# A graph network's gathers: one tile by single-row transfers before, two tiles and half of a third after, shared by two queues

## The reference

```python
h = relu(layernorm(x)); h = h @ enc_w + enc_b; h_list = [h]
for l in range(3):
    e = edge_attr @ edge_w[l] + edge_b[l]              # 16 -> 128
    msg = relu(h_list[l][src] + e)                     # a gather of 212,500 rows
    agg = segment_sum(msg, dst, num_segments=n_nodes)
    z = (1.0 + eps[l]) * h_list[l] + agg
    z = relu(z @ mlp_w1[l] + mlp_b1[l]) @ mlp_w2[l] + mlp_b2[l]
    h_list.append(relu(z))
out = x + (concatenate(h_list, axis=1) @ out_w + out_b)
```

## Time and profile before

| | us |
|---|---|
| median of 3 runs | 6243.44 |
| lowest, highest | 6243.08, 6244.88 |
| the profiled execution | 6233.49 |
| its span | 6231.7 |
| busy PE, PEld | 4832.8, 3004.4 |
| busy POOL | 4667.1 |
| busy DVE, ACT | 1645.1, 987.6 |

### The profile page before, as it was taken

The page is one execution under the profiler, slowest core; times in us unless marked ns, Lnnn a source line. Parts: engine busy times, 40 slices in busy tenths (PEclk is TensorE's granted clock), DMA queues, the critical chain, the costliest instruction groups (busy, mean ns, idle before and its releaser), DMA issues.

```text
span 6231.7 us, 86632 instructions
## 1 busy us (share of the span) xinstructions
PE 4832.8 (78%) x14396; PEld 3004.4 (48%) x14397; DVE 1645.1 (26%) x4181; ACT 987.6 (16%) x1583; POOL 4667.1 (75%) x4998
## 2 busy tenths in 40 slices
PE   7887777777777777777777777777777777777777
PEld 5554444444444444444444444444444444444444
DVE  6322222222222222222222222222222222222222
ACT  4111111111111111111111111111111111111111
POOL 6777777777777677777777777767777777777776
PEclk8555555555555555555555555555555555555555
DMA  4222222222222222222222222222222222222223
GB/s 140 66 64 64 62 64 64 64 64 62 64 64 64 63 63 64 63 63 64 64 64 64 62 64 64 64 62 61 60 61 61 61 61 60 61 61 60 59 60 96
DMA packets 209009, 408.00 MB, mean 65 GB/s; under 512 B 93779, under 2 KB 106684, under 8 KB 207948
## 3 DMA queue, kind: packets, MB, share of 16 engines
q0 software_dynamic: 156960, 321.77, 19.8%
q10 hardware_dynamic: 22096, 59.87, 3.3%
q1 hardware_dynamic: 29508, 22.58, 1.1%
HBM read 378.16 MB, written 25.69 MB: 65 GB/s over the span
## 4 chain that ended last, share of the span: by engine, by line
POOL 40%; PE 22%; issue 15%; DMA 14%; DVE 5%; ACT 4%; DVEq 0%; POOLq 0%; ACTq 0%
POOL rows L383 40%; DMA rows<-h_table,idx 14%; PE bank L634 14%; PE bank L630 6%; DVE rows L887 4%; ACT rows L551 4%; PE bank L653 0%; PE bank L655 0%; PE bank L608 0%; PE bank L600 0%; DVE onehot L751 0%; DMA out_acc<-x_t 0%; PE bank L593 0%; DVEq L957 0%; PE bank L661 0%
## 5 line engine op out<-in xcount | busy, mean ns | idle before, releaser
L383 POOL DMA_INDIRECT rows<-h_table,idx x4905 | 4630.1, 944 | 1525.8 <-issue 1266.7
L634 PEld LDWEIGHTS bank<-onehot,rows 128*128 128x128 f32 x9966 | 2087.3, 306 | 2784.9 <-ACT rows L551 2659.0
L634 PE MATMUL bank<-onehot,rows 128*128 128x64 f32 x9966 | 2235.3, 400 | 1347.8 <-ACT rows L551 1347.0
L630 PE MATMUL bank<-edgew,attr 65*128 65x512 f32 x2496 | 2235.2, 1008 | 9.3 <-DMA w2s<-w 9.3
L887 DVE TENSOR_TENSOR rows<-bank,rows 128x512 f32<-128x512 f32 x1248 | 861.0, 690 | 4037.0 <-DMA rows<-h_table,idx 3913.5
L551 ACT ACTIVATE rows<-rows 128x512 f32<-128x512 f32 x1248 | 784.3, 628 | 5156.6 <-DVE rows L887 5156.6
L630 PEld LDWEIGHTS bank<-edgew,attr 65*128 65x128 f32 x2496 | 665.0, 310 | 270.2 <-issue 270.2
L873 DVE TENSOR_TENSOR onehot<-bank,dst_rel 128x256 f32<-128x256 f32 x1248 | 518.1, 415 | 204.7 <-issue 204.7
L883 DVE TENSOR_TENSOR agg_t<-bank,agg_t 128x64 f32 x1248 | 269.6, 216 | 288.6 <-PE bank L634 288.4
L653 PE MATMUL bank<-agg_t,w1s 128*128 (+1 forms) x150 | 149.2, 1098 | 1.5 <-DVE agg_t L883 1.5
L674 PE MATMUL bank<-outw,h_t 128*128 128x128 f32 x588 | 148.8, 396 | 0.7 <-ACT h_t L514 0.7
(11 more groups left out here) (82 smaller groups left out, 459.6 us busy)
## 6 DMA issues: line engine op xcount, KB each, us to landing
rows<-h_table SPq DMA_DIRECT2D x9984, 0.5 KB
rows<-h_table,idx POOLq DMA_INDIRECT x4905, 2.5
attr<-ea_t ACTq DMA_DIRECT2D x155, 256.0 KB, 3.6
h_table<-h_n ACTq DMA_DIRECT2D x48, 256.0 KB, 2.1
h_table<-rows SPq DMA_DIRECT2D x24, 256.0 KB, 2.7
out<-out_acc SPq DMA_DIRECT2D x24, 256.0 KB, 3.1
out_acc<-x_t ACTq DMA_DIRECT2D x4, 1280.0 KB, 16.7
rows<-dst_g SPq DMA_DIRECT2D x1, 832.0 KB
```

The source lines that it names most:

```text
L383: return g.indirect_dma_start(dst, None, h_table[l % 2], bass.IndirectOffsetOnAxis(ap=index, axis=0))
L630: return nc.tensor.matmul(dst[0:EP, 0:tiles * D], cols, edgew[:, l, 0:tiles * D], start=True, stop=True)
L634: last = nc.tensor.matmul(dst[:, 0:WIN], rows[0:EP, slot, j, :], onehot[0:EP, hot_slot, j, :], start=(j == 0), stop=(j == tiles - 1))
```

## The change

- The row numbers come as `row_at`, three rows of them for three tiles of each round, and DVE multiplies them by 512 once, ahead of `s_ready`. The registers then hold byte addresses, and the table is seen as bytes (`h_bytes`), so that no address is computed for a row.
- SP now brings 176 rows of a round: rows 0 to 47 of the fourth tile of group 13, and all 128 of the fourth tile of group 14, in chunks of 16 with a load of 16 registers ahead of each.
- ACT brings 144 rows of a round, behind its relus, in chunks of at most 12: rows 48 to 127 of group 13's tile behind the relus of groups 0 to 6, and rows 64 to 127 of the fourth tile of group 15 behind those of groups 7 to 12. The last round has no such part of group 15.
- POOL gathers 62 tiles in a full round instead of 63, one of them with 64 rows.
- DVE waits for `shared_fetched`, `sync_fetched` and `half_fetched` at groups 13, 14 and 15.
- The 24 results of layer 2 are written to `out` by ACT, behind the relu of group 5 of each half (`store_out`), no longer by SP at the end. ACT waits for the end of the layer before (`stored`) ahead of each layer's first group.

```diff
-FK, FJ = 14, 3
-LOADS = 32
+SYNC_GROUP, SHARED_GROUP = 14, 13
+SHARED_BY_SYNC = 48
+CHUNK = 16
+ACT_ROWS = 12
+HALF_GROUP = 15
+BY_POOL = 64
...
+        def table_row(l, eng, at):
+            byte = eng.snap(at, donate=True, min_val=0, max_val=(NR * P - 1) * (D * 4))
+            return h_bytes[l % 2][bass.ds(byte, D * 4)].rearrange("(a d) -> a d", a=1)
...
-                def fetch_tile(b):
-                    for first in range(0, EP, LOADS):
-                        sp.load(row, row_idx[0:1, bass.ds(b * EP + first, LOADS)])
-                        for i in range(LOADS):
-                            at = sp.snap(row[i], min_val=0, max_val=NR * P - 1)
-                            sp.dma_start(rows[first + i:first + i + 1, FK, FJ, :], table[bass.ds(at, 1), :])\
-                              .then_inc(fetched, 16)
+                def fetch_rows(b, u, group, count, fetched):
+                    for first in range(0, count, CHUNK):
+                        with ExitStack() as held:
+                            at = [held.enter_context(sp.register(f"sync_at{next(named)}")) for _ in range(CHUNK)]
+                            sp.load(at, row_at[u:u + 1, bass.ds(b * EP + first, CHUNK)])
+                            for i in range(CHUNK):
+                                row = rows[first + i:first + i + 1, group, TG - 1, :]
+                                sp.dma_start(row.bitcast(u8), table_row(l, sp, at[i])).then_inc(fetched, 16)
+
+                def fetch_body(b):
...
+                    freed(SHARED_GROUP)
+                    fetch_rows(b, 1, SHARED_GROUP, SHARED_BY_SYNC, shared_fetched)
+                    freed(SYNC_GROUP)
+                    fetch_rows(b, 0, SYNC_GROUP, EP, sync_fetched)
...
-            with sp.Fori(0, ND) as i:
-                sp.wait_ge(o_added, i + ((L - 1) * NU + 1 + N0))
-                sp.dma_start(out[:, bass.ds(i * (UT * D), UT * D)].rearrange("p (t d) -> p t d", d=D),
-                             out_acc[:, bass.ds(i * UT, UT), :]).then_inc(s_out, 16)
...
-                    tiles = min(TG, NTR - group * TG) - (slot == FK)
-                    if slot != FK and tiles < TG:
+                    tiles = min(TG, NTR - group * TG)
+                    if slot in (SYNC_GROUP, SHARED_GROUP):
+                        tiles = TG - 1
+                    elif tiles < TG:
...
-                        gather(l, rows[0:EP, slot, t % TG, :], idx[0:EP, t:t + 1]).then_inc(gathered[slot], 16)
+                        here = BY_POOL if slot == HALF_GROUP and t % TG == TG - 1 else EP
+                        gather(l, rows[0:here, slot, t % TG, :], idx[0:here, t:t + 1]).then_inc(gathered[slot], 16)
...
+                def fetch_some(b, k):
+                    shared = -(-(EP - SHARED_BY_SYNC) // ACT_ROWS)
+                    if k < shared:
+                        first = SHARED_BY_SYNC + k * ACT_ROWS
+                        fetch_rows(b, 1, SHARED_GROUP, first, min(first + ACT_ROWS, EP), shared_fetched)
+                    elif not isinstance(b, int):
+                        first = BY_POOL + (k - shared) * ACT_ROWS
+                        if k == shared:
+                            wait_apart(act, agg_done, b * RING + (l * NG + HALF_GROUP + 1 + S0 - RING))
+                        if first < EP:
+                            fetch_rows(b, 2, HALF_GROUP, first, min(first + ACT_ROWS, EP), half_fetched)
...
+                        if k == 0 and not (isinstance(b, int) and b == 0 and l == 0):
+                            wait_apart(act, agg_done, b * RING + (l * NG + SHARED_GROUP + 1 + S0 - RING))
+                        fetch_some(b, k)
+
+                act.wait_ge(stored, l * NU * 16 + 16)
...
+                dve.wait_ge(row_at_in, 48)
+                own(v.tensor_scalar(row_at[:, :], row_at[:, :], float(D * 4), None, ALU.mult))
                 dve.sem_inc(s_ready, 1)
```

More of the change, by code:

```diff
@@ L3 @@
 from contextlib import ExitStack
+import itertools
 P = 128
@@ L54, in gnn_kernel @@
     assert ND * UT + LAST == -(-nodes // P) and NB == -(-NG // HB) and NGP <= P * GR and NI <= NBU
-    assert REST == RING and FK < RING - 1 and EP % LOADS == 0
+    assert REST == RING and EP % CHUNK == 0 and SHARED_BY_SYNC % CHUNK == 0
+    assert (EP - SHARED_BY_SYNC) // ACT_ROWS + 1 < SHARED_GROUP < SYNC_GROUP < HALF_GROUP == RING - 1 and GL < TG
     h_table = [nc.dram_tensor(f"h_table{u}", (NR * P, D), f32).ap() for u in range(2)]
@@ L59, in gnn_kernel @@
     h_last = [h[ND * UC:NR * P, :].rearrange("(p j) d -> p (j d)", j=LAST) for h in h_table]
+    h_bytes = [h.rearrange("n d -> (n d)").bitcast(u8) for h in h_table]
     spans_dram = nc.dram_tensor("spans", (2, NGP), i32).ap()
@@ L307, in _ @@
                     sp.dma_start(outb[:, :], out_b.partition_broadcast(P)).then_inc(s_par, 16)
-            row = [sp.alloc_register(f"row{i}") for i in range(LOADS)]
+            named = itertools.count()
             for l in range(L):
-                table = h_table[l % 2]
                 def far_pass():
@@ L317, in far_pass, with freed @@
                         sp.dma_start(far_attr[0:KA - 1, :], ea_t[:, bass.ds(g * EP, EP)]).then_inc(f_attr, 16)
-                def fetch_tile(b):
-                    for first in range(0, EP, LOADS):
-                        sp.load(row, row_idx[0:1, bass.ds(b * EP + first, LOADS)])
-                        for i in range(LOADS):
-                            at = sp.snap(row[i], min_val=0, max_val=NR * P - 1)
-                            sp.dma_start(rows[first + i:first + i + 1, FK, FJ, :], table[bass.ds(at, 1), :])\
-                              .then_inc(fetched, 16)
+                def fetch_rows(b, u, group, count, fetched):
[7 more added lines that the diff above has]
+                def fetch_body(b):
+                    def freed(group):
+                        before = l * NG + group + 1 + S0 - RING
+                        if not isinstance(b, int):
+                            wait_apart(sp, agg_done, b * RING + before)
+                        elif b or l:
+                            sp.wait_ge(agg_done, b * RING + before)
+                    freed(SHARED_GROUP)
+                    fetch_rows(b, 1, SHARED_GROUP, SHARED_BY_SYNC, shared_fetched)
+                    freed(SYNC_GROUP)
+                    fetch_rows(b, 0, SYNC_GROUP, EP, sync_fetched)
                 if l == 0:
@@ L491, in _ @@
             n_far = load_extra(act)
+            for u in range(4):
+                act.wait_ge(p_stored[u], (NI + 3 - u) // 4 * 16)
+            named = itertools.count()
             def load_weights(l):
@@ L515, in relu_h, with store_out @@
                       .then_inc(h_ready, 1)
+                def store_out(i):
+                    act.wait_ge(o_added, i + (l * NU + 1 + N0))
+                    act.dma_start(out[:, bass.ds(i * (UT * D), UT * D)].rearrange("p (t d) -> p t d", d=D),
+                                  out_acc[:, bass.ds(i * UT, UT), :]).then_inc(s_out, 16)
                 def store(i):
@@ L541, in load_next_attr, with fetch_rows @@
                            .then_inc(attr_in[1 - half], 16)
+                def fetch_rows(b, u, group, first, stop, fetched):
+                    with ExitStack() as held:
+                        at = [held.enter_context(act.register(f"act_at{next(named)}")) for _ in range(first, stop)]
+                        act.load(at, row_at[u:u + 1, bass.ds(b * EP + first, stop - first)])
+                        for i in range(first, stop):
+                            row = rows[i:i + 1, group, TG - 1, :]
+                            act.dma_start(row.bitcast(u8), table_row(l, act, at[i - first])).then_inc(fetched, 16)
+                def fetch_some(b, k):
[9 more added lines that the diff above has]
+                            fetch_rows(b, 2, HALF_GROUP, first, min(first + ACT_ROWS, EP), half_fetched)
                 def edge_body(b, groups):
@@ L553, in edge_body @@
                             load_next_attr(b, half)
-                        if kk in (2, 3, 5)[:3 if l < L - 1 else 2] and groups - half * HB >= HB:
+                        if kk in (2, 3, 5) and groups - half * HB >= HB:
                             with act.If(unit > 0):
-                                (relu_z if kk == 2 else relu_h if kk == 3 else store)(unit_before(unit))
+                                (relu_z if kk == 2 else relu_h if kk == 3 else
+                                 store if l < L - 1 else store_out)(unit_before(unit))
+                        if k == 0 and not (isinstance(b, int) and b == 0 and l == 0):
+                            wait_apart(act, agg_done, b * RING + (l * NG + SHARED_GROUP + 1 + S0 - RING))
+                        fetch_some(b, k)
+                act.wait_ge(stored, l * NU * 16 + 16)
                 with act.Fori(0, NFULL) as b:
```

39 lines of the change are left out of this document (20 added, 19 removed).

## The result

| | before | after |
|---|---|---|
| median of 4 runs, us | 6244.16 | 6296.41 |
| lowest, highest | 6243.08, 6246.46 | 6294.53, 6299.0 |
| span of the profiled execution | 6231.7 | 6292.7 |

The ratio is 1.0083 [1.0066, 1.0101]: the change makes the kernel 0.8% slower, where 1.1% faster was forecast. The interval leaves out 1, so the loss is clear, small as it is. Both kernels were measured once more later, on another chip: 6308.19 against 6233.47, 1.0129 [1.011, 1.0148].

A forecast was written before the change was run, and what follows sets the result against it. POOL's gathers were taken to bound the kernel. Layer 0 at +9 and layers 1 and 2 at -38.6 each made -68 on 6233.5, so 6165.5, and 9.9 more for the median: 6175 us, range 6120 to 6300.

The forecast's parts named there:

- The bound of before: Old kernel: POOL's gathers, 1.249 us each, 63 a round, set the pace; POOL a ring ahead, SP waiting 12.4 us a round.
- POOL's ceiling: POOL's round: one gather fewer (1.249 us), the gather of 64 rows at 0.70, giving 77.17 us; 38.6 saved a layer.
- The second rival: POOL's gather of 64 rows costs as much as one of 128: 18 us back, 6193 us; chance 0.06.
- SP: SP's 176 rows: 0.340 us a row, 1.25 a load of 16 registers, 77.3 us a round (73.7 to 78.8).
- The third rival: SP sets the pace at 78.7 us a round, through a load of 1.39 or a row of 0.347: 6286 us; chance 0.13.
- ACT: ACT's 144 new rows: 66.8 us of work plus 8.9 from relu 13 to the next round's relu 0, 75.7 a round.
- the fourth rival: ACT sets the pace at 78.8 us a round, through a load of 1.06 or a row of 0.347: 6314 us; chance 0.22.
- Layer 0: First layer loses its catching up: first group at 135.5 us, then rounds of 76.5, ending at 2122 against 2113, 9 us longer.
- the table's 3.8 us: Start of layer 0: DVE multiplies three rows of 3328 numbers by 512 ahead of `s_ready`, 3.8 us more.
- Other edits: Stores of `out` on ACT cost 0.9 us each, as in layers 0 and 1; taking SP's away and waiting for `stored` change nothing.
- What was to show it: Signs in the profile of after: L402's minimum 0.47 to 0.94, POOL's slot waits over 0.3 us if another engine sets the pace.
- the forecast's own case: POOL keeps the pace at 77.17 us a round in layers 1 and 2, layer 0 gets 9 us longer: 6175 us; chance 0.42.

The follow-up runs named there:

- f1: The changed kernel with POOL gathering group 15's fourth tile whole and ACT fetching rows only behind groups 0 to 6: 6149.0 us against 6241.79 for before, 0.985.
- e4: The changed kernel with POOL gathering group 15 whole and ACT fetching no rows (rows 48 to 127 of group 13's tile left out): 10146.31 us, 1.0071 against before's 10074.12.
- e3: The changed kernel with ACT's 144 rows in chunks of 16 instead of 12, on the slower kind of chip: 8557.72 us, 0.8498 against before's 10074.12.

## Why the prediction was wrong

**The bound of before** was read rightly: 1.249 us a gather, a ring of lead, SP with 12.4 us to spare. f1, which again runs at 62 gathers a round, confirms the price: 77.4 forecast by it, 77.3 to 77.8 measured in layers 1 and 2.

**POOL's ceiling** missed by the gather of 64 rows: 0.907 instead of 0.70, so that POOL's round is 77.4 and not 77.2. The second rival had this right as a price. It cost nothing in the end, since POOL didn't set the pace; but it means that the half tile, which brings ACT 64 rows a round, could spare POOL no more than 0.04 us. The middle between 0.47 and 0.944 was a choice without a row.

**SP** was right in kind and a little dear: the load 1.144 (forecast 1.25), a row 0.330 (0.340), the round 75.4 in layer 0 of f1 (77.3). The third rival, SP's pace at 78.7, has fallen. In after SP still waits 280.8 / 72 = 3.9 us a round for its slots, but the consumers do come up to it: at group 14 DVE waits for single rows 41 times, 87.2 us in all, up to 2.9 us in rounds 1 to 8 and 18 to 24 and up to 8.3 in the last round of a layer, where ACT has no more than 80 rows.

**ACT** is the step that failed. Its round was put at 75.7, under POOL's, and is 78.9. By terms: groups 0 to 12 68.2 for 66.8, the rest 10.7 for 8.9. In the first part a row was right (0.32 in the mean for 0.325), but the load took 0.957 for 0.82, and the first transfer of each chunk 0.24 more than the others, 13 times a round, a term that my sum put at nothing. The earlier trace rows has a small transfer (L467) at 0.22 and the large one of `attr` at 0.48, a difference that I didn't ask about. These two terms alone are nearly 5 us a round (1.7 and 3.1). The cheaper row takes 0.6 back, and about 3 of what I had added up, by this balance, cost nothing: the timeline has the node network's arithmetic (L530) beside the load and the transfers. In the second part DVE's two register loads and the one-hot ahead of the first add were missing from the chain: 2.1 us between DVE's last sum and its add, where I had 1.3 for all of DVE. The other 1.0 us of the second part isn't taken apart.

So the fourth rival came true, *ACT sets the pace*, with Q = 78.8 and 6314 (measured 78.9 and 6296.41), though its reason was in part another: the load of 12 is not 1.06. What it argued with did happen in kind: ACT's loads of one register went from 0.28 in the median before to 0.49 in after. Its split by layers holds as well: +67, +2, +2 forecast, +55, -5, +6 measured. What I got wrong was to put it at 0.22. The forecast had ACT 1.5 us under POOL's pace, with a row, a load and a chain each estimated and none of them shown beside a relu; four estimates that could each be off by 0.1 to 2 us don't leave a margin of 1.5. The measured 6296.41 lies within 6120 to 6300, but not by the forecast's mechanism: the range went up that far to take in half of this rival.

**Layer 0** is the term by which the sign turned: +9 forecast, +55 measured. The mechanism was as told, no catching up, and the size is 25 rounds by the pace: 78.7 in the mean of all 25 for 76.5, which is 55 us too few. Two smaller terms were too large and take 8 back: the table's 3.8 us didn't show, as the first add came only 0.9 later than before (132.6, forecast 135.5), and the last round took 68.4 for 74. In layers 1 and 2 a round is about 1.6 us over the forecast's 77.17, which takes the 38.6 that each was to save.

**Other edits.** A store in ACT's stream isn't free where ACT sets the pace. In rounds 9 to 17 of every layer a round is 80 us, and 76.9 to 79.2 else: there `relu_z` and `store` (in layer 2 the stores of `out`) fall behind groups 2 and 5, where ACT has no slack, and the gap behind group 5 is 6.5 to 6.6 instead of 5.3 to 5.4 us. In the other rounds they fall behind groups 10 to 13, close to the pause. The stores of `out` cost there what those to `h_table` cost in layers 0 and 1, as the forecast had it. And the end of the kernel got 2 us longer behind the last add, where I had zero.

**What was to show it** did: L402's minimum between 0.47 and 0.94 (0.902), the relus that wait for nothing in groups 1 to 13, DVE waiting for PE's sums. POOL's waits for slots over 0.3 us came in layer 0, where it begins a ring ahead (44 of them); in layers 1 and 2 it begins with the others, the ring doesn't fill, and POOL pauses at the end of the layer. A second queue that issues didn't make the other's transfers longer: SP's stay at 225 ns. Relus that wait for nothing, and DVE waiting for PE's sums, were written down for the forecast's own case, so they don't tell it from the fourth rival; POOL's waits for slots do.

**A margin of the rules.** The Trainium skill, "DMA: Bandwidth & Descriptors", section "Latency and other measured facts", has about 600 ns as the floor of a `tensor_load`. The load of 4 registers above took 484 ns, so the measurement decides against it, as I had assumed.

Left open: why the queues stand still on some chips, and why less so the more rows ACT takes; what makes the first transfer of a chunk dear on ACT, and every second load of ten registers; what bytes alone, an earlier load, and no rows on ACT would do on the chips of the first kind.

## What to carry to other kernels

Where a queue gets extra instructions between its arithmetic, add up two parts apart: the groups that carry them, at that queue's own pace, and the groups that carry none, at the pace of the chain through all engines, since idle time in these can't be lent to the others. Here, on chips of the first kind, the rows that fit, 80 behind groups 0 to 6, gained 1.5%, and 64 more turned that into a loss of 0.8%: f1 (0.985) is the version to keep there, and it beats both kernels. On chips of the second kind the order was another (f1 0.953, chunks of 16 0.850), so the kind of chip comes first. Before a gather is cut in half, see whether its price depends on its rows at all.

## What the runs showed of the hardware

- An indirect gather of 64 rows of 512 bytes took 0.91 us, one of 128 rows 0.94, each with 0.30 ahead of it: between these two the price is nearly fixed.
- A load of registers took, in the median, 0.28 us for 1 register (ACT), 0.48 for 4, 0.72 for 8, 0.96 for 12, 1.14 (SP) and 1.20 (ACT) for 16, 2.04 for 32; but 1.00 to 1.17 and 2.34 to 2.70 by turns for ten, from places 40 bytes apart. What stands ahead counts too: ACT's loads of 12 took 0.79 behind groups 0 and 8, 1.14 behind 1 and 9, where the transfer of `attr` stands right ahead, and 0.96 else; its load of 1 took 0.28 before and 0.49 in after.
- The first transfer of a chunk of rows took 0.46 us on ACT, the next ones 0.22, with the registers loaded ahead of the relu as well; on SP the first took 0.26.
- ACT's jump back at the end of its loop, with its body longer by 144 transfers, took 2.6 us (from 3202.24 to 3204.84, beside a wait for DVE that lasts longer). Over the kernel the pause behind the jump is 0.18 us in the median before (68 instructions a pass) and 2.5 in after (386); SP's, with 396 and 380 instructions, is 2.4 and 2.6. In f1 (244) ACT's is 0.22, but over 1 us in 24 of 75 jumps, those of layer 2. The queue that fetches instructions moved 799 packets in after and 429 before, and in each of ACT's 72 long pauses of after one of its packets of 8192 bytes starts, some 0.9 us behind the jump. The Trainium skill, "Runtime: NRT & Kernel Launch", section "Instruction fetch mechanics", says that a branch to code outside the fetched window must wait for a fetch; the trace agrees, as far as the packets and the pauses show it.
- On some chips the queues of SP and ACT stood still for 0.6 to 0.8 us at a time, SP's about once in 8 (e4) to 13 (e3) instructions. The kernel before took some 10,060 us there instead of 6,240, the kernel of f1 9,597 instead of 6,149, while the medians of the transfers and of the gathers stayed what they were.
